# VectorE takes the residual additions of a step between the products and the scans of the next unit

## Chip, cores and metric

The kernel runs on one core of a Trainium2 chip. The metric is the device time of one execution in microseconds (us); lower is better. Before the change the median of three runs is 1209.81 us (1209.77 to 1210.84).

## What is computed

A decoder layer on x of shape (4, 512, 512): a selective state-space block (Mamba), a cross-attention to a context, and an int8-quantized linear layer, each added to x and followed by a layer norm.

```python
proj = einsum('blh,he->bel', x, W_in); hidden, gate = split(proj)
hidden = silu(causal_conv(hidden) + conv_bias)
dt, Bm, Cm = split(hidden.T @ W_x)
dts = softplus(dt @ W_dt + b_dt)
dA  = exp(dts[..., None] * A);  dBu = dts[..., None] * Bm[:, :, None, :] * hidden[..., None]
state = dA[t] * state + dBu[t];  y[t] = einsum('ben,bn->be', state, C[t])      # 512 steps t
x = layernorm(x + ((y + hidden * D) * silu(gate)) @ W_out)
q, k = ctx @ Wq.T + bq, ctx @ Wk.T + bk
x = layernorm(x + x @ softmax(q @ k.T).T)
x = layernorm(x + dequantized(int8(x) @ int8(weight).T) + bias)
```

## The kernel before

**Units and steps.** A batch has E = 1024 channels with N = 16 states each. One unit is 32 channels with all their states: 128 partitions by NJ = 4 rows of T = 512. A batch has 32 units, so there are 128 in all. The program is a table of steps (b, g) with b from -1 to 4 and g from 0 to 31, and every engine walks the same table. In step (b, g) VectorE works on unit u = 32b + g + 1 of the scan; I call it the unit of step g of batch b.

**Five engines on a unit.** SyncE copies the step sizes and inputs of the unit to all partitions (`rep`, L358). ScalarE computes dA = exp (four instructions at L598, for the unit after the present one) and copies the inputs to PSUM (`du_rep`, L606), once VectorE has done the products of the unit before. VectorE multiplies `du_rep` by B into `dBu` (two instructions, L811, "the products") and scans (two instructions, L817). GpSimd multiplies the states by C (two instructions, L466). TensorE sums the states of four units into one product per 128 channels, the key `y` (L945 and L951, function `state_sum`, at g a multiple of 4). VectorE's `finish` (L795, at g = 1, 5, 9, ...) gates that sum.

**The ring.** The states lie in `st`, a ring of RING = 6 units. From the seventh unit on, VectorE's products of unit u wait until TensorE has summed the unit that lay there. For the unit of step g = 4m + 1 that is the sum `y` of step 4m, the step before.

**The dense work beside the scan.** Each step also has items, listed by `items(b, g)` from the tables REST, REST_BESIDE and REST_AFTER: products of TensorE that ScalarE, VectorE or both read. They belong to the batch before (output projection `wo`, scores `en`, attention `at` and `av`, int8 product `ff`), to the gate of the present batch (`g`), or to the batch after (`h`, `c`, `z`, `dt`, `bc`). The four residual kinds are `wo` (g = 2, 5, 6, 7), `av` (15, 17, 19, 21), `ff` (19, 21, 23, 25) and, in the last batch, the early part of its own output projection, `wp` (27 to 30). VectorE adds each of these products to a row block of x: one SCALAR_TENSOR_TENSOR with a row sum (L776, function `add_rows`), or TENSOR_TENSOR (L892) for `wp`; `ff` is scaled first (L903). After it, ScalarE takes the moments in the next step, GpSimd the rstd, and ScalarE normalizes. The numeral behind a kind is the row block: `wo3` is the fourth.

**Three banks.** All dense products share BANKS = 3 PSUM banks in strict turn, in the order of the items. TensorE starts product n only when product n - 3 has been read:

```python
def bank_of(key):
    slot, n = turn[key]
    if n:
        pe.wait_ge(s_free[slot], n)
    return bank(key), s_full[slot]
```

For a residual it is VectorE that gives the bank back, by `dve.sem_inc(free, 1)` behind the addition (L895 and L906). TensorE takes its items in order, so a product that waits for its bank holds up all behind it. For the residual `wo3` the product three places on is the state sum `y` of step 8. For the last batch's loop (b = 3, the dense work is batch 2's) the products three places behind `av0`, the first `ff` and the third `ff` are the state sums of steps 16 and 20 and the gate of step 23; in the loops b = 1 and 2 they are the state sums of steps 16, 20 and 24.

**VectorE's order in a step**, before: products and scans of the unit (`unit(u)`), `finish`, the norms' small parts, and then the items of the step in their order, residuals among them.

Of the kernel before, what the change touches and what calls it, by code (L numbers as in the profile page):

```python
# [5 lines left out]
ALU = mybir.AluOpType  # L6
# [6 lines left out]
NB = 4  # L13
# [13 lines left out]
UNITS = NE * NQ  # L27
TT = T // P
# [91 lines left out]
def decoder_layer(nc, x, xT, ctxT, w_in, w_conv, conv_k, conv_b, w_x, w_dt, b_dt, w_out, a_log, d_skip,  # L120
# [10 lines left out]
    with ExitStack() as ctx:  # L131
# [25 lines left out]
        ws_bc = sb("ws_bc", [P, H])  # L157
# [32 lines left out]
        rows_of = [x1[:]] * LAST + [hs_spare[:, KH:2 * KH, :]]  # L190
# [101 lines left out]
        def product_read(eng, key):  # L292
            slot, n = turn[key]
            eng.wait_ge(s_free[slot], n + 1)
# [458 lines left out]
        def _(dve):  # L753
            V = nc.vector
            chain = [0]

            def link(ins):

                chain[0] += 1
                ins.then_inc(s_chain, 1)  # L760
                dve.wait_ge(s_chain, chain[0])

            def full(key):
                product_done(dve, key)
                return bank(key), s_free[turn[key][0]]
# [5 lines left out]
            def add_rows(key, x_i, ps):  # L771

                n = norm[key]
                if n >= 4:
                    normalized(dve, norm_keys[n - 4])
                V.scalar_tensor_tensor(x_i, ps, 1.0, x_i, ALU.mult, ALU.add,  # L776
                                       accum_out=rowsum[:, n % 4:n % 4 + 1]).then_inc(s_sum, 1)
                dve.wait_ge(s_sum, n + 1)
# [18 lines left out]
                dve.wait_ge(s_y, NE * b + e + 1)  # L797
                dve.sem_inc(free, 1)  # L798

            def unit(u):  # L800
                dve.wait_ge(s_duf, u + 1)
                B = spread_at(dve, u, s_bb, 0, Bb)
                if u >= RING:

                    n = (u - RING) // NQ
                    product_done(dve, ("y", n // NE, n % NE))
                for h in range(NH):
                    j = slice(JH * h, JH * h + JH)
                    if u:
                        dve.wait_ge(s_scan, NH * (u - 1) + h + 1)  # L810
                    V.tensor_tensor(dBu[:, j, :], du_rep[:].unsqueeze(1).to_broadcast([P, JH, T]), B[:, j, :],  # L811
                                    ALU.mult).then_inc(s_mul, 1)
                for h in range(NH):
                    j = slice(JH * h, JH * h + JH)
                    dve.wait_ge(s_mul, NH * u + h + 1)
                    dve.wait_ge(s_dA, NJ * u + JH * (h + 1))
                    V.tensor_tensor_scan(st[:, u % RING, j, :].rearrange("p j t -> p (j t)"),  # L817
                                         dA[:, u % 2, j, :].rearrange("p j t -> p (j t)"),
                                         dBu[:, j, :].rearrange("p j t -> p (j t)"), 0.0,
                                         ALU.mult, ALU.add).then_inc(s_scan, 1)  # L820

            def quantize_weight():

# [24 lines left out]
            V.tensor_scalar(Aneg[:], Aneg[:], -1.0, None, ALU.mult).then_inc(s_prep, 1)  # L848

            norms = {}  # L850
            for s, (b, g) in enumerate(STEPS):
                if 0 <= UNITS * b + g + 1 < NB * UNITS:
                    unit(UNITS * b + g + 1)
                if b == -1 and g == 28:
                    quantize_weight()
                n = NE * b + g // 4 - 1
# [18 lines left out]
                        V.reciprocal(xinv[:, i:i + 1], sc).then_inc(s_xi, 1)  # L875
                for kind, kb, i in items(b, g):
                    key = (kind, kb, i)
                    x_i = rows_of[kb][:, i, :] if kind in ("wp", "wo", "av", "ff") else None
                    if kind == "h" and kb == 0:
                        hid_front(kb, i)  # L880
                    elif kind == "en":
                        ps, _ = full(key)
                        if i >= 2:
                            dve.wait_ge(s_ex, TT * kb + i - 1)
                        V.tensor_reduce(nmax[:, i % 2:i % 2 + 1], ps, AX_X, ALU.max, negate=True).then_inc(s_mx, 1)
                        norms.setdefault(s + 1, []).append(key)
                    elif kind in ("wp", "wo", "av"):
                        if kind in ("wp", "wo") and i == 0:
                            dve.wait_ge(s_xr, 16 * (kb + 1))
                        ps, free = full(key)  # L890
                        if kind == "wp":
                            link(V.tensor_tensor(x_i, ps, x_i, ALU.add))  # L892
                        else:
                            add_rows(key, x_i, ps)
                        dve.sem_inc(free, 1)  # L895
                        if kind == "av":
                            norms.setdefault(s + QUANT_LAG, []).append(key)
                    elif kind == "ff":
                        ps, free = full(key)
                        if kb == 0 and i == 0:  # L900
                            product_read(dve, ("ws", 0, 0))

                        link(V.scalar_tensor_tensor(ps, ps, xsc[:, i:i + 1], ws_bc[:], ALU.mult, ALU.mult))  # L903
                        dve.wait_ge(s_xb, TT * kb + i + 1)
                        add_rows(key, x_i, ps)
                        dve.sem_inc(free, 1)  # L906

        @block.tensor
        def _(pe):
# [187 lines left out]
```

## Time and profile before

| | |
|---|---|
| median of 3 runs | 1209.81 us |
| the profiled execution | 1212.85 us; span 1211.1 us |
| VectorE busy | 974.8 us, 80% |
| TensorE busy | 866.9 us, 72% |
| ScalarE busy | 855.8 us, 71% |
| GpSimd busy | 814.6 us, 67% |
| granted TensorE clock, mean | 0.856 of 2.4 GHz |

The span runs from the first to the last instruction, and the profiled execution's own time is 1.7 us above it. The scans of the 128 units lie between about 75 and 1155 us; before that come the first batch's projections, and behind it the last batch's dense work. In the rows, DVE is VectorE, ACT ScalarE, POOL GpSimd, PE TensorE, and a trailing q is an engine's instruction queue (its waits and semaphore updates).

### The profile page before, as it was taken

The page shows a single profiled execution, that of the slowest core. Times are in us where ns is not written, and L with a number is a line of the kernel's source. Part 1 is how long each engine was busy: PE and PEld are TensorE (multiplying, and loading weights), DVE is VectorE, ACT ScalarE, POOL GpSimd, SP SyncE. Part 2 cuts the span into 40 slices and gives each one's busy share as a digit, 9 for nine tenths or more (in the row PEclk, how much of TensorE's full clock was granted, in tenths as well). Part 3 has the DMA queues.
Part 4 walks back from the last instruction along what each step waited for, and adds up shares of the span by engine and source line. Part 5 has one row for each costly group of instructions (what it writes and reads, how often), then busy time and mean ns, then how long its engine had stood idle before and what let it go on. Part 6 is the DMA issues. An engine that isn't in the chain of part 4 may idle for free.

```text
span 1211.1 us, 10560 instructions
## 1 busy us (share of the span) xinstructions
PE 866.9 (72%) x2718; PEld 339.3 (28%) x2718; DVE 974.8 (80%) x783; ACT 855.8 (71%) x1458; POOL 814.6 (67%) x515
## 2 busy tenths in 40 slices
PE   7933488878368789877549788896727946675995
PEld 2221133322023233332114233332202312222331
DVE  2459999987789987778888977887788999999733
ACT  2386777766557887786666886878756788787546
POOL 2238888876667776686767766868766777777533
PEclk9966699988679889988869899998977978778996
DMA  5184444442973334242793332443395353225100
GB/s 172 35 183 113 97 113 113 126 112 55 244 196 74 87 97 112 70 122 74 186 271 91 85 97 73 103 117 92 89 249 165 72 140 87 59 70 156 27 0 35
DMA packets 66684, 135.03 MB, mean 111 GB/s; under 512 B 13120, under 2 KB 19392, under 8 KB 66624
## 3 DMA queue, kind: packets, MB, share of 16 engines
q1 hardware_dynamic: 65904, 134.28, 43.5%
q8 instruction: 22, 0.36, 0.1%
q14 instruction: 38, 0.31, 0.1%
q10 hardware_dynamic: 720, 0.08, 0.0%
HBM read 62.75 MB, written 4.46 MB: 55 GB/s over the span
## 4 chain that ended last, share of the span: by engine, by line
PE 27%; issue 24%; ACT 18%; DVE 18%; DMA 5%; POOL 4%; SPq 2%; DVEq 0%; ACTq 0%; POOLq 0%
PE dense L919 18%; DVE st L817 12%; PE dense L974 6%; ACT dA L598 5%; POOL st L466 3%; DMA rep<-steps 2%; DVE dBu L811 2%; PE dense L951 2%; DMA wide<-w_out 1%; ACT squares L629 1%; DVE hs L795 1%; SPq L358 1%; ACT du_rep L606 1%; ACT tb L588 1%; PE dBu L929 1%
## 5 line engine op out<-in xcount | busy, mean ns | idle before, releaser
L466 POOL TENSOR_TENSOR st<-st,Cb 128x1024 f32<-128x1024 f32 x250 | 584.4, 2359 | 180.9 <-DVE st L817 153.5
L817 DVE TENSOR_TENSOR_SCAN st<-dA,dBu 128x1024 f32<-128x1024 f32 x256 | 570.2, 2269 | 0.3 <-ACT dA L598 0.3
L598 ACT ACTIVATE dA<-rep,Aneg 128x511 f32<-128x511 f32 x512 | 327.7, 710 | 82.0 <-DMA rep<-steps 51.6
L811 DVE TENSOR_TENSOR dBu<-du_rep,Bb 128x1024 f32<-128x1024 f32 x250 | 294.6, 1224 | 91.8 <-ACT du_rep L606 60.6
L919 PE MATMUL dense<-xTs,Win 128*128 128x512 f32 x512 | 242.2, 618 | 16.6 <-DMA xTs<-xT 7.7
L919 PE MATMUL dense<-wide,hs 128*128 128x512 f32 x256 | 122.2, 634 | 57.9 <-DVE hs L795 34.3
L919 PEld LDWEIGHTS dense<-xTs,Win 128*128 128x128 f32 x512 | 99.1, 198 | 154.2 <-issue 153.5
L974 PE MATMUL dense<-pj,Win 128*128 128x512 f32 (+1 forms) x192 | 106.1, 704 | 47.0 <-DVEq L798 21.2
L951 PE MATMUL dense<-st,sel 128*32 128x512 f32 x1024 | 124.3, 629 | 2.9 <-POOL st L466 2.9
L606 ACT COPY du_rep<-rep 128x512 f32<-128x512 f32 x128 | 74.4, 581 | 41.2 <-DVE dBu L811 39.4
L945 PE MATMUL dense<-hs,Ddiag 128*128 128x512 f32 x64 | 41.2, 731 | 81.9 <-ACT Ddiag L676 72.2
L511 POOL TENSOR_TENSOR ta<-ta,tb 128x512 f32<-128x512 f32 x32 | 41.1, 1284 | 73.5 <-ACT tb L714 71.3
L919 PEld LDWEIGHTS dense<-wide,hs 128*128 128x128 f32 x256 | 51.2, 204 | 127.3 <-issue 65.0
L497 POOL TENSOR_TENSOR steps<-tb,ta 128x512 f32<-128x512 f32 x32 | 40.6, 1270 | 54.4 <-ACT tb L588 54.4
L974 PEld LDWEIGHTS dense<-pj,Win 128*128 128x128 f32 x192 | 42.6, 231 | 108.3 <-issue 108.3
L480 POOL TENSOR_TENSOR hs<-tb,ta 128x512 f32<-128x512 f32 x32 | 40.7, 1272 | 39.6 <-ACT tb L558 39.6
L937 PE MATMUL dense<-ident,small 128*128 128x128 f32 x128 | 25.2, 333 | 46.7 <-ACT small L647 26.7
L951 PEld LDWEIGHTS dense<-st,sel 128*32 128x32 f32 x1024 | 31.1, 116 | 97.5 <-issue 84.8
L711 ACT ACTIVATE tb<-dense 128x512 f32<-128x512 f32 x32 | 18.9, 592 | 55.1 <-PE dense L919 54.7
L776 DVE SCALAR_TENSOR_TENSOR x<-dense,x 128x512 f32<-128x512 f32 x36 | 24.7, 687 | 36.1 <-PE dense L919 29.0
L919 PE MATMUL dense<-hs,wide 128*128 128x512 f32 x80 | 43.6, 702 | 10.3 <-issue 9.6
L472 POOL TENSOR_TENSOR rstd<-var,neghalf 128x1 f32<-128x1 f32 x48 | 26.5, 551 | 36.0 <-ACT var L632 36.0
(117 smaller groups left out, 998.4 us busy)
## 6 DMA issues: line engine op xcount, KB each, us to landing
rep<-steps SPq DMA_DIRECT2D x512, 128.0 KB, 2.7
Win<-w_in SPq DMA_DIRECT2D x64, 256.0 KB, 2.7
wide<-w_out SPq DMA_DIRECT2D x4, 2048.0 KB, 14.0
Win<-w_conv SPq DMA_DIRECT2D x24, 256.0 KB, 2.7
wide<-bc_rows SPq DMA_DIRECT2D x24, 256.0 KB, 6.5
xTs<-xT SPq DMA_DIRECT2D x4, 1024.0 KB, 10.9
Bb<-bc_rows SPq DMA_DIRECT2D x16, 256.0 KB, 10.8
Cb<-bc_rows SPq DMA_DIRECT2D x16, 256.0 KB, 11.8
```

Source lines behind the costliest of these rows:

```text
L466: nc.gpsimd.tensor_tensor(s, s, C[:, j, :], ALU.mult).then_inc(s_p, 1)
L480: nc.gpsimd.tensor_tensor(hs[:, kb % 2, i, :], tb[:, m, :], ta[:, m, :], ALU.mult).then_inc(s_hs, 1)
L497: nc.gpsimd.tensor_tensor(steps[:, n % 3, 0, :], t, a, ALU.add).then_inc(s_dt, 1)
L511: nc.gpsimd.tensor_tensor(a, a, t, ALU.mult).then_inc(s_gate, 1)
L598: nc.scalar.activation(dA[:, u % 2, j, 1:T], rep[:, u % REPS, 0, 1:T], ACT.Exp, scale=Aneg[:, u % UNITS, j:j + 1]).then_inc(s_dA, 1)
L606: nc.scalar.copy(du_rep[:], rep[:, u % REPS, 1, :]).then_inc(s_duf, 1)
L811: V.tensor_tensor(dBu[:, j, :], du_rep[:].unsqueeze(1).to_broadcast([P, JH, T]), B[:, j, :], ALU.mult).then_inc(s_mul, 1)
L817: V.tensor_tensor_scan(st[:, u % RING, j, :].rearrange("p j t -> p (j t)"), dA[:, u % 2, j, :].rearrange("p j t -> p (j t)"), dBu[:, j, :] ...
L919: mm = nc.tensor.matmul(ps[0:rows, :], lhsT, rhs, start=n == 0, stop=n == len(pairs) - 1)
L945: nc.tensor.matmul(ps, Ddiag[:], hs[:, b % 2, e, :], start=True, stop=False)
L951: mm = nc.tensor.matmul(ps[32 * q:32 * q + 32, :], sel[:, 0:32], st[:, (4 * n + q) % RING, j, :], start=False, stop=j == NJ - 1)
L974: mm = nc.tensor.matmul(ps[:, k:T], Win[:, n % 3, k, :], pj[:, 0:T - k], start=k == 0, stop=k == KC - 1)
```

## The change

`unit` is split into `products` and `scans`. An item of a residual kind is no longer done in its place: its key goes into the list `late`, and the next step does it between the products and the scans of its unit. Steps without a unit (the tail behind the last scan) do it at their start. The other engines' programs are the same, instruction by instruction.

```diff
-            def unit(u):
+            def products(u):
                 dve.wait_ge(s_duf, u + 1)
                 B = spread_at(dve, u, s_bb, 0, Bb)
                 if u >= RING:
...
+
+            def scans(u):
+
                 for h in range(NH):
...
+            def residual(key):
+
+                kind, b, i = key
+                x_i = rows_of[b][:, i, :]
+                if kind in ("wp", "wo") and i == 0:
+                    dve.wait_ge(s_xr, 16 * (b + 1))
+                ps, free = full(key)
+                if kind == "wp":
+                    link(V.tensor_tensor(x_i, ps, x_i, ALU.add))
+                elif kind == "ff":
...
+                    link(V.scalar_tensor_tensor(ps, ps, xsc[:, i:i + 1], ws_bc[:], ALU.mult, ALU.mult))
+                    dve.wait_ge(s_xb, TT * b + i + 1)
+                    add_rows(key, x_i, ps)
+                else:
+                    add_rows(key, x_i, ps)
+                dve.sem_inc(free, 1)
...
+            late = []
             for s, (b, g) in enumerate(STEPS):
                 if 0 <= UNITS * b + g + 1 < NB * UNITS:
-                    unit(UNITS * b + g + 1)
+                    products(UNITS * b + g + 1)
+                for key in late:
+                    residual(key)
+                late = []
+                if 0 <= UNITS * b + g + 1 < NB * UNITS:
+                    scans(UNITS * b + g + 1)
...
-                    elif kind in ("wp", "wo", "av"):
...
+                    elif kind in ("wp", "wo", "av", "ff"):
+                        late.append(key)
                         if kind == "av":
                             norms.setdefault(s + QUANT_LAG, []).append(key)
-                    elif kind == "ff":
...
```

VectorE's order before, from step 6 to step 9 of the loop b = 1: L811 are the products, L817 the scans, L776 the residuals `wo2` (bank dense1) and `wo3` (bank dense0), L885 the score maximum of `en0`.

```order
L811 TENSOR_TENSOR dBu<-du_rep,Bb 128x1024 x2
L817 SCALAR_TENSOR_TENSOR st<-dA,dBu 128x1024 x2
L776 SCALAR_TENSOR_TENSOR x1,rowsum<-dense1,x1 128x512
L811 TENSOR_TENSOR dBu<-du_rep,Bb 128x1024 x2
L817 SCALAR_TENSOR_TENSOR st<-dA,dBu 128x1024 x2
L776 SCALAR_TENSOR_TENSOR x1,rowsum<-dense0,x1 128x512
L811 TENSOR_TENSOR dBu<-du_rep,Bb 128x1024 x2
L817 SCALAR_TENSOR_TENSOR st<-dA,dBu 128x1024 x2
L885 TENSOR_REDUCE nmax<-dense2 128x1
```

And in the changed kernel, over the same steps (the scans now have line L820, the score maximum L913):

```order
L811 TENSOR_TENSOR dBu<-du_rep,Bb 128x1024 x2
L776 SCALAR_TENSOR_TENSOR x1,rowsum<-dense1,x1 128x512
L820 SCALAR_TENSOR_TENSOR st<-dA,dBu 128x1024 x2
L811 TENSOR_TENSOR dBu<-du_rep,Bb 128x1024 x2
L776 SCALAR_TENSOR_TENSOR x1,rowsum<-dense0,x1 128x512
L820 SCALAR_TENSOR_TENSOR st<-dA,dBu 128x1024 x2
L913 TENSOR_REDUCE nmax<-dense2 128x1
L811 TENSOR_TENSOR dBu<-du_rep,Bb 128x1024 x2
L820 SCALAR_TENSOR_TENSOR st<-dA,dBu 128x1024 x2
```

Each residual has moved past the two products of the next unit, and so has the return of its bank.

The second place is the turn from step 23 to step 24 of the loop b = 3. Before, VectorE scales and adds the third `ff` (bank dense2), takes two score maxima, and then does the products:

```order
L903 SCALAR_TENSOR_TENSOR dense2<-dense2,xsc,ws_bc 128x512
L776 SCALAR_TENSOR_TENSOR x1,rowsum<-dense2,x1 128x512
L885 TENSOR_REDUCE nmax<-dense0 128x1
L885 TENSOR_REDUCE nmax<-dense1 128x1
L811 TENSOR_TENSOR dBu<-du_rep,Bb 128x1024 x2
L817 SCALAR_TENSOR_TENSOR st<-dA,dBu 128x1024 x2
```

In the changed kernel (L838 is the scaling):

```order
L913 TENSOR_REDUCE nmax<-dense0 128x1
L913 TENSOR_REDUCE nmax<-dense1 128x1
L811 TENSOR_TENSOR dBu<-du_rep,Bb 128x1024 x2
L838 SCALAR_TENSOR_TENSOR dense2<-dense2,xsc,ws_bc 128x512
L776 SCALAR_TENSOR_TENSOR x1,rowsum<-dense2,x1 128x512
L820 SCALAR_TENSOR_TENSOR st<-dA,dBu 128x1024 x2
```

The third `ff` now stands behind the maxima and behind the products of step 24.

## Rows read from the trace of the kernel before

**Rows 1.** The page, part 4: the chain that ended last, shares by engine.
```profile
PE 27%; issue 24%; ACT 18%; DVE 18%; DMA 5%; POOL 4%; SPq 2%; DVEq 0%; ACTq 0%; POOLq 0%
```

**Rows 2.** Waits of VectorE: who waited for whom: us in total, times, longest.
```profile
DVE x L776 <- PE dense L919: 29.0, 5, 7.2
DVE dense L903 <- PE dense L919: 14.7, 6, 4.8
```

**Rows 3.** Timeline of VectorE, b = 1, steps 2 to 17: start, us, instruction, [idle before].
```profile
352.72 0.69 DVE L776 SCALAR_TENSOR_TENSOR x<-dense,x 128x512 f32<-128x512 f32 x1 [2.86 <-PE dense L919]
...
353.67 2.37 DVE L811 TENSOR_TENSOR dBu<-du_rep,Bb 128x1024 f32<-128x1024 f32 x2 [0.24 <-PE dense L919]
355.94 4.45 DVE L817 TENSOR_TENSOR_SCAN st<-dA,dBu 128x1024 f32<-128x1024 f32 x2
361.71 2.36 DVE L811 TENSOR_TENSOR dBu<-du_rep,Bb 128x1024 f32<-128x1024 f32 x2 [1.31 <-ACT du_rep L606]
...
473.03 2.36 DVE L811 TENSOR_TENSOR dBu<-du_rep,Bb 128x1024 f32<-128x1024 f32 x2 [0.72 <-PE dense L951]
```

**Rows 4.** Timeline of VectorE, b = 1, steps 7 to 9.
```profile
391.89 0.67 DVE L776 SCALAR_TENSOR_TENSOR x<-dense,x 128x512 f32<-128x512 f32 x1
...
393.01 2.36 DVE L811 TENSOR_TENSOR dBu<-du_rep,Bb 128x1024 f32<-128x1024 f32 x2 [0.44 <-ACT du_rep L606]
...
400.23 2.35 DVE L811 TENSOR_TENSOR dBu<-du_rep,Bb 128x1024 f32<-128x1024 f32 x2
```

**Rows 5.** Timeline of TensorE, b = 1, the state sum of step 8.
```profile
392.68 2.07 PE L945 MATMUL dense<-hs,Ddiag 128*128 128x512 f32 x2 [2.94 <-DVEq L895]
394.68 4.11 PE L951 MATMUL dense<-st,sel 128*32 128x512 f32 x32
```

**Rows 6.** Chain in order of time, b = 2, steps 7 to 9.
```profile
679.75 2.07 PE dense L945 x2
681.82 5.56 PE dense L951 x32
...
687.51 0.10 DVE dBu L811
```

**Rows 7.** Timeline of ScalarE: its copies to du_rep behind residuals, b = 1 and 3.
```profile
526.39 0.59 ACT L606 COPY du_rep<-rep 128x512 f32<-128x512 f32 x1 [1.18 <-DVE dBu L811]
...
1079.62 0.59 ACT L606 COPY du_rep<-rep 128x512 f32<-128x512 f32 x1 [1.67 <-DVE dBu L811]
```

**Rows 8.** Timeline of TensorE, b = 3: state sums of steps 16 and 20, gate of step 23.
```profile
1027.61 3.64 PE L951 MATMUL dense<-st,sel 128*32 128x512 f32 x32
...
1060.72 3.64 PE L951 MATMUL dense<-st,sel 128*32 128x512 f32 x32
...
1093.07 3.67 PE L919 MATMUL dense<-xTs,Win 128*128 128x512 f32 x8 [2.08 <-DVEq L906]
```

**Rows 9.** Timeline of VectorE, b = 3, steps 15 to 29.
```profile
1026.69 2.36 DVE L811 TENSOR_TENSOR dBu<-du_rep,Bb 128x1024 f32<-128x1024 f32 x2 [0.24 <-ACT du_rep L606]
...
1033.33 2.34 DVE L811 TENSOR_TENSOR dBu<-du_rep,Bb 128x1024 f32<-128x1024 f32 x2
...
1056.92 0.69 DVE L776 SCALAR_TENSOR_TENSOR x<-dense,x 128x512 f32<-128x512 f32 x1
...
1066.16 2.34 DVE L811 TENSOR_TENSOR dBu<-du_rep,Bb 128x1024 f32<-128x1024 f32 x2
...
1091.39 0.74 DVE L903 SCALAR_TENSOR_TENSOR dense<-dense,xsc,ws_bc 128x512 f32<-128x512 f32 x1
...
1094.64 2.36 DVE L811 TENSOR_TENSOR dBu<-du_rep,Bb 128x1024 f32<-128x1024 f32 x2 [0.34 <-ACT du_rep L606]
...
1140.33 2.36 DVE L811 TENSOR_TENSOR dBu<-du_rep,Bb 128x1024 f32<-128x1024 f32 x2 [3.83 <-PE dense L951]
```

**Rows 10.** Timeline of ScalarE, b = 3: du_rep of step 19, gate of step 23.
```profile
1057.39 0.58 ACT L606 COPY du_rep<-rep 128x512 f32<-128x512 f32 x1
...
1097.14 0.60 ACT L711 ACTIVATE tb<-dense 128x512 f32<-128x512 f32 x1 [0.17 <-ACT xTs L739]
```

More of the change, by code:

```diff
@@ L820, in unit @@
                                          ALU.mult, ALU.add).then_inc(s_scan, 1)
+            def residual(key):
[7 more added lines that the diff above has]
+                elif kind == "ff":
+                    if b == 0 and i == 0:
+                        product_read(dve, ("ws", 0, 0))
+                    link(V.scalar_tensor_tensor(ps, ps, xsc[:, i:i + 1], ws_bc[:], ALU.mult, ALU.mult))
[4 more added lines that the diff above has]
+                dve.sem_inc(free, 1)
             def quantize_weight():
@@ L877, in _ @@
                     key = (kind, kb, i)
-                    x_i = rows_of[kb][:, i, :] if kind in ("wp", "wo", "av", "ff") else None
                     if kind == "h" and kb == 0:
@@ L886, in _ @@
                         norms.setdefault(s + 1, []).append(key)
-                    elif kind in ("wp", "wo", "av"):
[L888 to L895, printed above, removed]
+                    elif kind in ("wp", "wo", "av", "ff"):
+                        late.append(key)
                         if kind == "av":
                             norms.setdefault(s + QUANT_LAG, []).append(key)
-                    elif kind == "ff":
[L899 to L906, printed above, removed]
         @block.tensor
```

## Prediction

> **What bounds the kernel now.** I read the views in this order: the chain that ended last, VectorE's waits, then the timelines of VectorE, TensorE and ScalarE at every residual. No engine bounds the span alone: the chain is shared by TensorE, ScalarE and VectorE, with "issue" for the rest [rows 1]. VectorE's waits for the product that a residual adds come to 29.0 + 14.7 us [rows 2]. So each step ends on whichever wait is last there, and the change has to be priced place by place. There are 52 residuals; 12 lie in the tail, where no unit is left and VectorE's order stays the same, and one more (the last `wp`) is followed by a step without a unit. The other 39 stand at 33 turns of a step.
>
> **What the change moves.** No instruction is added. A residual that started right behind the scans now starts 2.27 us after the next products start, since 355.94 - 353.67 is what the products hold VectorE [rows 3]. A plain residual takes 0.95 us of VectorE (353.67 - 352.72) [rows 3]. The products are issued earlier, the residual later, the scans as before if both were ready. Nothing is moved past SyncE's or GpSimd's queue. Three things can then happen.
>
> **1. A wait for TensorE is covered.** `wo0` in three loops, `av0` twice, `av2`/`ff0` twice and the third `ff` twice wait for their product longer than the products take: 2.86 us in the row shown, up to 7.2 [rows 2, 3]. There the scans start about 2.3 us earlier, nine times. But what the next step waits for is not VectorE's. Behind `wo0` the next products already wait 1.31 us for `du_rep` [rows 3], which ScalarE copies only after it has read TensorE's later products; behind `av0` they wait 0.72 us for the state sum [rows 3], and I take the two `ff` places to be alike. I cost this gain at nothing; what covers it is TensorE's own run of products, and if that were faster the whole 2.3 us would count.
>
> **2. ScalarE gets its copy earlier.** Where ScalarE was waiting for VectorE's products, the products now come before the residual. Behind `av3`/`ff1` the copy waited 1.18 us in the loops b = 1 and 2 and 1.67 us in b = 3 [rows 7], and there the chain runs through ScalarE. Gain 2 x 1.18 = **2.4 us** in the first two; the third is used in item 3. The bounds are 0 and 2.4: nothing else of size waits there.
>
> **3. The bank comes back later, and TensorE waits.** This is the term that decides. The release goes from the end of the residual before the products to 2.27 us and one residual after their start. Where `n + 3` starts later than that anyway it costs nothing: `wo0`, `av1`, `av3`, `ff1`, all of `av0`, `ff0`, `ff2` in the first two loops, and `wo1`/`wo2`, whose delay only moves products that ScalarE or VectorE come to later still. It costs at these places:
>
> State sum of step 8, three loops. TensorE already stood idle 2.94 us for the bank of `wo3` and began 0.79 us after the residual did (392.68 - 391.89) [rows 4, 5]. Now the products start when `du_rep` is there, 393.01; the residual at 395.28; the sum at 396.07, 3.39 us later. It ended at 394.68 + 4.11 = 398.79 and will at 402.2. By the ring the products of step 9 need it: 402.3 instead of 400.23, +2.1 us. In b = 2 the sum was already what those products waited for (679.75 to 687.38, then 687.51) [rows 6], so all 3.4 us count. The same sum took 6.1 us in one loop and 7.6 in the other [rows 5, 6], so lengths are unsure: if each takes 7.6, it is 3.6 + 3.4 + 3.6 = 10.6; if each takes 6.1, it is 2.1 + 1.9 + 2.1 = 6.1. The loop b = 3 has rows as b = 1. I take **8.2**, near the middle, since I have one row of each length.
>
> State sum of step 16, b = 3. The release lay just before the products at 1026.69 [rows 9] and goes 3.0 us back. The sum ended at 1031.25 [rows 8] and will at 1034.3; the next products started at 1033.33 [rows 9] and will at 1034.4: +1.0. If the sum takes 7.6 us as in rows 6 instead of its 4.7 here, +3.9. I take **1.9**.
>
> State sum of step 20, b = 3. The pair began at 1056.92 [rows 9]. Now the products begin with `du_rep`, copied by 1057.97 [rows 10], and the pair at 1060.24, 3.3 us later. The sum ended at 1064.36 [rows 8], will at 1067.7, and the next products come at 1067.7 instead of 1066.16 [rows 9]: I take **1.4**, bounds 1.0 and 4.0 by the same slower sum.
>
> Gate of step 23, b = 3. TensorE waited 2.08 us for the bank of the third `ff` and started at 1093.07 [rows 8]; ScalarE read the gate at 1097.14, just as it was full [rows 10]. Now the products wait for `du_rep` until 1094.64, and the `ff` starts at 1096.91 instead of 1091.39 [rows 9]: 5.5 us later, and the gate is in front of ScalarE's next exps and copy. The 1.67 us of item 2 bring `du_rep` forward, of which I keep 1.1, because the norm there also waits for GpSimd. Net 4.4. Bounds: 3.5, if the whole head start counts and a little slack is left, and 7.6, if the gate's 3.67 us double at half clock. I take **4.5**.
>
> `wp1`, b = 3. It was done in a 3.83 us wait for the state sum [rows 9]; behind the products it delays the scans by its whole **0.95 us**, bounds 0.9 and 2.6 (its bank). Small ones at the third loop's `ff3`: 0.3.
>
> Sum: 8.2 + 1.9 + 1.4 + 4.5 + 0.95 + 0.3 - 2.4 = **+14.9 us**. With all lower ends (6.1 + 1.0 + 1.0 + 3.5 + 0.9 - 2.4) it is +10.1, with all upper ends and no gain (10.6 + 3.9 + 4.0 + 7.6 + 2.6 + 0.3) +29.0.
>
> **The clock.** The state sum at 392.68 came after 2.94 us of TensorE standing idle and took 6.1 us, the one at 679.75 took 7.6 [rows 5, 6]; the one at 1060.72 ran at 3.64 us for its L951 part, against 5.56 [rows 6, 8]. The change makes the idle stretches longer, hence the slower ends above. The Trainium skill ("TensorE: Matmul & The Clock Gate", section "What's actually happening") says that the throttled clock is the default and that activity releases it. By that rule every delayed product would run at the lower clock, and the sum would be near the +29 of the upper ends; the row of 6.1 us agrees only in part.
>
> **Rivals.**
> *A, the queue is cleared (faster).* VectorE's queue is in order, so a residual whose product is late holds products that are ready. If ScalarE's copy follows VectorE's products closely after `wo0`, `av0`, `ff0` and `ff2`, each of the nine places gives 2.3 us and the gains of item 2 are kept: -20.7 - 2.4 = -23, or 1186.8 us. It decides as soon as `du_rep` of the next unit comes over 2.3 us earlier than now. For it: 43.7 us of such waits [rows 2]. Against: `du_rep` is the later one behind `wo0` [rows 3]. The Trainium skill states the same order ("TensorE: Matmul & The Clock Gate", "Architectural detail: the array is 16× 32×32, not 1× 128×128"): VectorE's queue is strictly first in, first out. By that rule alone the change wins.
> *B, the banks are not felt (no change).* TensorE's delay is absorbed by slack that the chain does not show. Then only VectorE's own shifts remain: three times 0.9 us behind `wo3` (the residual no longer fills the 0.44 us wait and what lay before it), 0.8 and 1.1 at steps 15 and 19, 0.95 at `wp1`, minus 2.4 and the rest of item 2: +1.5, or 1211.3 us. For it: step 9 had 1.4 us of slack in b = 1. Against: the chain of b = 2 goes through that very sum [rows 6], and TensorE was waiting for the release [rows 5].
> *C, everything slower.* The low clock holds after each new gap: +25 to +29, about 1237. The Trainium skill ("Perfetto Trace Analysis", section "Matmuls") wants products to rotate through banks so that reading one overlaps the next; here the reading is put off with only three banks. It speaks for my sign, not for a size.
> That the change does nothing is ruled out: the order of 39 residuals is different.
>
> **How the numbers follow.** The forecast has 0.72, A 0.07, B 0.13, C 0.08. The profiled execution took 1212.85 us, 3.0 above the median; its sum gives 1227.8, and against the median of 1209.81 us it is 1224.7 us. About 0.2% (2.4 us) is what the measurement can tell from no change. The range must leave out at most 2 in 10: it drops A and most of B at the low end and most of C at the top, 1212 to 1232. Faster: A and a sliver of B, 0.08. Same: most of B, 0.11. Slower: 0.81.
>
> **What would show it.** Right: TensorE's idle time before L945 behind VectorE's release grows; the products of step 9 wait for L951 in all three loops; the state sum of step 8 starts over 3 us later relative to the end of the scans of step 7; VectorE's waits for L919 at the residuals shrink by up to 20 us while its waits for `du_rep` or L951 grow by more; between steps 22 and 25 of b = 3 the changed kernel loses 4 us or more; the tail behind 1166 us is as long as before. Wrong: if TensorE's waits for VectorE's release don't grow, or if steps 7 to 10 take as long as before, item 3 fails.

## The result, and the profile after

The changed kernel took 1228.28 us (median of 4 runs, 1224.77 to 1229.41), the kernel before beside it 1210.32 us (4 runs, 1209.77 to 1211.04): ratio 1.0143, 95% interval 1.0121 to 1.0165, so **slower by 18.0 us**. The forecast was 1224.7 us, with a range of 1212 to 1232.

The two profiled executions lie closer together, 1224.77 against 1212.85 us: that of the changed kernel is its fastest run, and that of the kernel before is longer than all its others here. They already differ by 3.8 us at the first products of b = 1, where both programs are still the same. Counted from there the change costs 15.7 us in the traces.

The chain that ended last, of the changed kernel (the page, part 4), against [rows 1]:

```profile
PE 29%; issue 22%; ACT 19%; DVE 15%; POOL 6%; DMA 6%; SPq 2%; DVEq 0%; ACTq 0%; POOLq 0%
```

VectorE went down by three points and TensorE up by two. VectorE's waits (us in total, times, longest):

```profile
DVE dBu L811 <- ACT du_rep L606: 93.8, 44, 8.8
...
DVE dBu L811 <- issue: 14.3, 4, 8.0
DVE dBu L811 <- PE dense L963: 13.4, 8, 3.0
...
DVE x L776 <- PE dense L931: 6.0, 5, 1.5
DVE dense L838 <- PE dense L931: 5.6, 5, 3.3
```

The last two answer to [rows 2]: VectorE now waits 11.6 us for late products and not 43.7. The change does what it says. But it waits elsewhere: 93.8 us for ScalarE's copy (63.8 before) and 13.4 us for the state sum, L963 (5.3 before). The reason is on TensorE. Its waits for VectorE's signal that a bank is free (L843 is the residual's `sem_inc`):

```profile
PE dense L931 <- DVEq L843: 17.7, 9, 8.4
PE dense L957 <- DVEq L843: 15.8, 6, 4.1
```

Before, the state sum waited 9.7 us for such signals. The state sums of step 8, in the order of the loops (TensorE's timeline: start, us, instruction, [idle before]):

```profile
391.95 2.08 PE L957 MATMUL dense<-hs,Ddiag 128*128 128x512 f32 x2 [4.07 <-DVEq L843]
393.95 5.69 PE L963 MATMUL dense<-st,sel 128*32 128x512 f32 x32
...
682.54 2.07 PE L957 MATMUL dense<-hs,Ddiag 128*128 128x512 f32 x2 [4.07 <-DVEq L843]
684.54 5.46 PE L963 MATMUL dense<-st,sel 128*32 128x512 f32 x32
...
968.57 2.07 PE L957 MATMUL dense<-hs,Ddiag 128*128 128x512 f32 x2 [4.08 <-DVEq L843]
970.57 4.11 PE L963 MATMUL dense<-st,sel 128*32 128x512 f32 x32
```

TensorE stands idle 4.1 us in front of each, 2.94 us before in b = 1 [rows 5]. VectorE around the first of them:

```profile
388.87 2.36 DVE L811 TENSOR_TENSOR dBu<-du_rep,Bb 128x1024 f32<-128x1024 f32 x2 [1.05 <-ACT du_rep L606]
391.15 0.68 DVE L776 SCALAR_TENSOR_TENSOR x<-dense,x 128x512 f32<-128x512 f32 x1
...
392.05 4.46 DVE L820 TENSOR_TENSOR_SCAN st<-dA,dBu 128x1024 f32<-128x1024 f32 x2 [0.21 <-DVE x L776]
...
399.78 2.36 DVE L811 TENSOR_TENSOR dBu<-du_rep,Bb 128x1024 f32<-128x1024 f32 x2 [2.68 <-issue]
```

The residual starts 2.28 us after the products and the sum 0.80 us after the residual, as the working had it. The sum ends at 399.64, and the next products at 399.78 stood 2.68 us idle for it. In [rows 4] they had nothing to wait for.

The gate of step 23 in b = 3, on TensorE's timeline:

```profile
1101.22 5.39 PE L931 MATMUL dense<-xTs,Win 128*128 128x512 f32 x8 [8.41 <-DVEq L843]
```

VectorE around it:

```profile
1097.26 2.37 DVE L811 TENSOR_TENSOR dBu<-du_rep,Bb 128x1024 f32<-128x1024 f32 x2 [0.60 <-ACT du_rep L606]
1099.53 0.75 DVE L838 SCALAR_TENSOR_TENSOR dense<-dense,xsc,ws_bc 128x512 f32<-128x512 f32 x1
...
1111.60 2.36 DVE L811 TENSOR_TENSOR dBu<-du_rep,Bb 128x1024 f32<-128x1024 f32 x2 [5.80 <-ACT du_rep L606]
```

ScalarE, where it reads the gate:

```profile
1106.65 0.60 ACT L711 ACTIVATE tb<-dense 128x512 f32<-128x512 f32 x1 [7.06 <-PE dense L931]
```

These answer to the last rows of [rows 8, 9, 10]: idle time of 2.08 us became 8.41, and the gate took 5.39 us, not 3.67, at a granted clock of 0.67, where it had been 1.00. ScalarE, which read it without waiting for TensorE, now waits 7.06 us, and behind it VectorE waits 5.80.

`wp1` and `wp2`, near the end of b = 3: TensorE now waits 2.60 us for the bank that `wp2` takes, where before it went on at once (24 matmuls here are `wp2` and `wp3` together):

```profile
1154.32 10.68 PE L931 MATMUL dense<-wide,hs 128*128 128x512 f32 x24 [2.60 <-DVEq L843]
```

Where the time went, in us, by the difference (after minus before) of the moment at which a unit's first product ended. "Lost" is the change of that difference over the stretch:

| stretch | difference | lost | forecast |
|---|---|---|---|
| first products of b = 1 | -3.8 | | |
| step 8 to 9, b = 1 | -4.1 to -0.4 | 3.7 | 2.1 to 3.6 |
| rest of b = 1 | -0.4 to -0.4 | 0 | -1.2 |
| step 8 to 9, b = 2 | -0.6 to 2.6 | 3.2 | 1.9 to 3.4 |
| rest of b = 2 | 2.6 to -0.4 | -3.0 | -1.2 |
| step 8 to 9, b = 3 | -0.6 to 1.5 | 2.1 | 2.1 to 3.6 |
| to step 17, b = 3 | 1.5 to 2.6 | 1.1 | 1.9 |
| to step 21, b = 3 | 2.6 to 4.0 | 1.4 | 1.4 |
| step 23 to 25, b = 3 | 4.0 to 9.7 | 5.7 | 4.5 |
| from there to the tail | 9.7 to 11.8 | 2.2 | 1.25 |

### The profile page after: what moved, and what is told of

Same layout as the page of the kernel before. It is cut to its first block, busy times and chain, and to the rows that moved or that the text cites. A ratio compares the mean times of both kernels' runs of the same rounds, so it can differ in the third digit from the quotient of the medians.

```text
span 1222.9 us, 10550 instructions
## 1 busy us (share of the span) xinstructions
PE 864.8 (71%) x2708; PEld 338.0 (28%) x2718; DVE 976.5 (80%) x783; ACT 855.8 (70%) x1458; POOL 814.6 (67%) x515
## 3 DMA queue, kind: packets, MB, share of 16 engines
HBM read 62.75 MB, written 4.46 MB: 55 GB/s over the span
## 4 chain that ended last, share of the span: by engine, by line
PE 29%; issue 22%; ACT 19%; DVE 15%; POOL 6%; DMA 6%; SPq 2%; DVEq 0%; ACTq 0%; POOLq 0%
PE dense L931 18%; DVE st L820 9%; ACT dA L598 6%; PE dense L986 6%; POOL st L466 4%; PE dense L963 3%; DVE dBu L811 3%; DMA wide<-w_out 2%; ACT du_rep L606 1%; DMA rep<-steps 1%; ACT squares L629 1%; ACT tb L588 1%; DMA Bb<-bc_rows 1%; DVE hs L795 1%; PE dense L957 1%
## 5 line engine op out<-in xcount | busy, mean ns | idle before, releaser
L820 DVE TENSOR_TENSOR_SCAN st<-dA,dBu 128x1024 f32<-128x1024 f32 x256 | 570.4, 2269 | 7.4 <-DVE x L776 6.4
L811 DVE TENSOR_TENSOR dBu<-du_rep,Bb 128x1024 f32<-128x1024 f32 x250 | 294.5, 1224 | 139.8 <-ACT du_rep L606 90.4
L963 PE MATMUL dense<-st,sel 128*32 128x512 f32 x1024 | 126.0, 636 | 2.9 <-POOL st L466 2.9
L963 PEld LDWEIGHTS dense<-st,sel 128*32 128x32 f32 x1024 | 31.3, 116 | 98.9 <-issue 85.5
L639 ACT ACTIVATE x<-x,nmean,rstd 128x512 f32<-128x512 f32 x36 | 28.9, 814 | 37.3 <-POOL nmean L474 37.3
L931 PE MATMUL dense<-wide 128*128 128x512 f32 x96 | 48.0, 646 | 3.6 <-ACT ta L584 2.5
## 6 DMA issues: line engine op xcount, KB each, us to landing
wide<-w_out SPq DMA_DIRECT2D x4, 2048.0 KB, 14.9
Cb<-bc_rows SPq DMA_DIRECT2D x16, 256.0 KB, 11.8
```

The lines of the kernel that those rows point to most:

```text
L931: mm = nc.tensor.matmul(ps[0:rows, :], lhsT, rhs, start=n == 0, stop=n == len(pairs) - 1)
L963: mm = nc.tensor.matmul(ps[32 * q:32 * q + 32, :], sel[:, 0:32], st[:, (4 * n + q) % RING, j, :], start=False, stop=j == NJ - 1)
```

## The experiments

All versions ran in three jobs, each beside the kernel before: its medians there were 1210.22 us (13 runs), 1211.08 us (19 runs) and 1211.81 us (27 runs), with single runs from 1206.51 to 1217.22. The versions that move some residuals only are the changed kernel with a condition in its last loop:

```diff
-                        late.append(key)
+                        if b < NB and (CONDITION):
+                            late.append(key)
+                        else:
+                            residual(key)
```

where `kb` is the batch of the residual, one less than the loop: `kb < LAST - 1` means the loops b = 1 and 2.

### Only the release is late

The kernel before, with this in place of `dve.sem_inc(free, 1)` behind a residual:

```diff
-                        dve.sem_inc(free, 1)
+                        late.append(free)
...
             def unit(u):
...
+                if late:
+                    dve.wait_ge(s_mul, NH * (u + 1))
+                    returned(late)
                 for h in range(NH):
```

> Every residual stays in its old place behind the scans; only the signal that gives its bank back is sent behind the next unit's products. Theory (the late bank is what costs): the state sum of step 8 and the gate of step 23 in b = 3 start late as in the changed kernel, less the 0.95 us of the residual itself: about 6.5 us for the three state sums, 4.6 us for the gate, 1 to 2 us for the rest, together +12 us against the kernel before (+8 to +18), near 1222 us. Rival (what costs is that VectorE does the residual between products and scans, so that the scans start later): the order on VectorE is the old one, so within 2 us of the kernel before, 1210 us.

Measured: 1225.48 us (4 runs, one of them 1236.2, which widens the interval), ratio 1.0164 (1.0113 to 1.0216). The scans kept their place behind the products, and the time was lost all the same. The edit does one thing more than delay the signal: VectorE waits for the signal of its own products, and so the scans start 2.57 us after the products start, not 2.27:

```profile
375.94 2.36 DVE L816 TENSOR_TENSOR dBu<-du_rep,Bb 128x1024 f32<-128x1024 f32 x2
378.51 4.47 DVE L825 TENSOR_TENSOR_SCAN st<-dA,dBu 128x1024 f32<-128x1024 f32 x2 [0.21 <-DVE dBu L816]
```

From these products to the next ones it took 7.66 us, and 7.56 before. At 33 turns that is 3.3 us at the most, too little for the 15.3. TensorE's waits in this version (L802 is the release, L956 the state sum's first products, L930 among others the gate, L948 products that transpose a block):

```profile
PE dense L930 <- DVEq L802: 16.3, 11, 6.5
PE dense L948 <- DVEq L802: 15.8, 7, 3.8
PE dense L956 <- DVEq L802: 12.3, 6, 3.4
```

The time between the medians is 15.3 us, for the change's 18.0. In the traces it is lost in the same places: 1.7, 1.5 and 1.7 us from step 8 to 9 of the three loops and 5.1 from step 23 to 25 of b = 3. So the rival, that the order of the work on VectorE alone costs the time, falls. It is not shown that the late signal is the whole of the change's loss: the three sums lose 4.9 us here and 9.0 there, where the residual stands in front of the signal as well (the sum starts 3.4 us later behind the scans of step 7, and 2.7 us here) and two of the sums also took longer.

### The release later still

```diff
-                if late:
-                    dve.wait_ge(s_mul, NH * (u + 1))
-                    returned(late)
...
+                    if h == 0 and late:
+                        dve.wait_ge(s_scan, NH * u + 1)
+                        returned(late)
```

> As the version in which only the signal that gives the bank back is late, but the signal now goes out behind the first of the next unit's two scans, 2.2 us later still; the residuals and everything else on VectorE in the old order. Theory: the three state sums, the gate of step 23 and the state sums of steps 16 and 20 of b = 3 start 2.2 us later once more, so 4 x 2.2 = 9 to 6 x 2.2 = 13 us above the first version, near 1236 us, more where slack in the loops b = 1 and 2 is used up. Rival (the cost is one lost turn, not a time that grows with the delay): as the first version, 1225 us.

Measured: 1253.36 us (4 runs), ratio 1.0336 (1.0307 to 1.0364), 41.5 us above the kernel before where 26 were expected. TensorE's waits for the same release:

```profile
PE dense L948 <- DVEq L802: 28.8, 7, 6.3
...
PE dense L930 <- DVEq L802: 24.5, 11, 8.5
PE dense L956 <- DVEq L802: 21.6, 8, 4.0
```

The cost grows with the delay, and faster than in proportion: 2.2 us more at each release turned 15.3 us into 41.5, each against the kernel before of its own job. The size was missed. From step 19 to 25 of b = 1 and b = 2 this version loses 6.4 and 8.8 us, where the first loses nothing; some of it comes back behind step 25. From step 9 to the next loop's first products it loses 4.1 and 5.7 us, where the first gains 1.9 and 0.4. So the clause "more where slack is used up", which had no number, carried 12 of the 28 us between the two traces; the other 16 are more than the 13 expected, too. How much of it is the lower clock (0.843 on the mean, 0.854 in the first version) stays open.

### Only wo

CONDITION `kind == "wo"`.

> Only the wo residuals go behind the next products; av, ff and wp stay in place. Theory: wo3 of three loops is in it and carries 8.7 us, wo0 to wo2 carry nothing; +8.7 us against the kernel before (+6 to +11), near 1219 us, and TensorE's idle time before the gate of step 23 in b = 3 is as before. Rival (each residual carries a like share, for instance through longer waits for du_rep): 11 of the 39 moved residuals, so 11/39 of the 18 us measured, +5 us or less.

Measured: 1219.30 us (4 runs), ratio 1.0085 (1.0062 to 1.0108): +9.1 us for an expected 8.7. Half of the loss comes from 12 of 39 residuals (the expectation counts 11, but there are four in each of three loops; the rival's +5 us would be 5.5). By the trace most of it comes from three of them: +2.2, +3.4 and +2.3 us from step 8 to 9 of the three loops, 7.9 together. From step 21 to 27 of b = 3, with the gate in it, the difference to the kernel before stays within 0.3 us.

### The third ff of b = 3 in its old place

CONDITION `key != ("ff", LAST - 1, 2)`.

> The changed kernel, but the third ff of the loop b = 3 stays behind the scans. Theory (its late bank holds up the gate of step 23): TensorE's idle time before that gate falls from 8.4 us to 2 to 4 us. If the gate then takes 3.67 us the whole 5.5 us come back, near 1223 us; if it takes 6.5 us, as it did with the chosen residuals alone behind 4.29 us of idle time, about 2.5 us come back, near 1226 us. Rival (the late av3/ff1 two steps before is what costs): no change, 1228 us.

Measured: 1226.78 us (4 runs, 1222.61 to 1231.93), ratio 1.0128 (1.0084 to 1.0172), 1.5 us below the changed kernel's 1228.28, which the scatter of the runs doesn't tell from nothing. In the trace the stretch from step 23 to 25 costs 3.1 us less, by the second branch of the expectation:

```profile
1062.84 2.08 PE L960 MATMUL dense<-hs,Ddiag 128*128 128x512 f32 x2 [0.93 <-DVEq L843]
1064.85 5.76 PE L966 MATMUL dense<-st,sel 128*32 128x512 f32 x32
...
1097.68 6.46 PE L934 MATMUL dense<-xTs,Win 128*128 128x512 f32 x8 [4.28 <-DVEq L843]
```

TensorE's idle time halved to 4.28 us, but the gate took 6.46 us. And the state sum of step 20, on which nothing was changed, took 7.8 us and not 4.7, which cost 3.1 us in this execution. So the gate's part is seen in the trace, and the medians neither show nor refute it.

### Chosen residuals

CONDITION `(kind, i) in (("wo", 0), ("av", 3), ("ff", 1)) or kb < LAST - 1 and (kind, i) in (("av", 0), ("av", 2), ("ff", 0), ("ff", 2))`, and in the second version all seven only with `kb < LAST - 1`.

> Moved are only the residuals whose product VectorE waits for longest and those behind which ScalarE waits for its copy, and none whose bank TensorE needs at once: wo0, av3 and ff1 in three loops, av0, av2, ff0 and ff2 in the loops b = 1 and 2 (wo0, av0, av2/ff0 and ff2 have late products). Theory (covered waits give nothing, the copy behind av3/ff1 gives 1.2 us a loop or somewhat more): -2 to -5 us against the kernel before, near 1206.5 us. Rival A of the prediction (VectorE's queue cleared at nine places gives 2.3 us each): of these, eight or nine places are in it, -15 us or more. Rival (these moves only lose): 0 or above.

> Moved are wo0, av0, av2, ff0, av3, ff1 and ff2 in the loops b = 1 and 2 only, nothing in b = 3. Theory: the gain of about 2.2 us a loop behind av3/ff1 stays and the 3.1 us that the earlier copy cost in b = 3 by a slow gate product are not there: -4 to -6 us against the kernel before, near 1205 us. Rival (the gains are the scatter of TensorE's clock): within 2 us of the kernel before.

Measured: the first 1208.24 us (10 runs), ratio 0.9983 (0.9962 to 1.0003), an interval that takes in no change; the second 1206.77 us (10 runs), ratio 0.9960 (0.9934 to 0.9987). The two intervals overlap, so that it is better to leave out b = 3 isn't shown by the medians. What speaks for it is the gate of b = 3, here in the first version:

```profile
1085.42 6.52 PE L934 MATMUL dense<-xTs,Win 128*128 128x512 f32 x8 [4.29 <-DVEq L843]
```

and the granted clock in the gate's stretch. The kernel before (window, its us, TensorE busy, PEclk, DMA share, GB/s):

```profile
1093.10:1096.60 3.50, 3.50 (x9) 1.00 1.01 344
```

The first version, in the same view:

```profile
1085.50:1091.80 6.30, 6.30 (x9) 0.55 1.06 336
```

The same eight matmuls at the same load of the DMA engines took 3.67 us at a granted clock of 1.00, which is 2.4 GHz, and 6.52 us at 0.55, mostly at 1.2 GHz. The earlier copy of ScalarE let TensorE run ahead into a wait of 4.29 us, not 2.08; the stretch from step 23 to 25 then lost 2.7 us in the trace. But in the second version, where nothing is moved in b = 3, the gate was slow too, at a granted clock of 0.67:

```profile
1084.73 5.37 PE L934 MATMUL dense<-xTs,Win 128*128 128x512 f32 x8 [2.51 <-DVEq L843]
```

It lost 1.4 us there. So a part of what the first version lost at its gate may be this scatter.

### Which of the chosen ones gain

Only av3 and ff1: CONDITION `kb < LAST - 1 and (kind, i) in (("av", 3), ("ff", 1))`. Only late products: the same with `wo0`, `av0`, `av2`, `ff0`, `ff2`.

> Only av3 and ff1 of step 21 go behind the next products, in the loops b = 1 and 2: four residuals. Theory (the gain of the chosen version is ScalarE's earlier copy, and the residuals with a late product give nothing): the same as that version, -3 to -5 us against the kernel before, near 1206.5 us. Rival A of the prediction (VectorE's queue, held by late products, is what is cleared): under half of it, 0 to -2 us.

> Only the residuals whose product VectorE waits for go behind the next products, in the loops b = 1 and 2: wo0, av0, av2, ff0 and ff2, at eight places of a step. Theory: what the next step waits for is not VectorE's, so each earlier scan is given back in the following step: 0, within 1.5 us of the kernel before. Rival A of the prediction: 2.3 us at each of the eight, up to -18 us; any part of it above 2 us speaks for it.

Measured: av3 and ff1 1208.13 us (11 runs), ratio 0.9974 (0.9951 to 0.9997), 3.7 us below the kernel before's 1211.81; the late products 1212.71 us (11 runs), ratio 0.9996 (0.9975 to 1.0016). The two intervals overlap a little, and the traces tell the two apart: from step 21 to 25 of b = 1 and b = 2, behind av3 and ff1, the first gains 2.3 and 2.0 us and the second nothing within 0.1, and over all that follows the first products of b = 1 the second gains 0.7 us. So four residuals bring the gain, and the ten others next to nothing. In the trace of the second, VectorE behind `wo0`:

```profile
345.74 2.34 DVE L811 TENSOR_TENSOR dBu<-du_rep,Bb 128x1024 f32<-128x1024 f32 x2
348.32 0.69 DVE L776 SCALAR_TENSOR_TENSOR x<-dense,x 128x512 f32<-128x512 f32 x1 [0.24 <-PE dense L934]
...
349.23 4.47 DVE L820 TENSOR_TENSOR_SCAN st<-dA,dBu 128x1024 f32<-128x1024 f32 x2 [0.21 <-DVE x L776]
357.30 1.23 DVE L811 TENSOR_TENSOR dBu<-du_rep,Bb 128x1024 f32<-128x1024 f32 x1 [3.61 <-ACT du_rep L606]
```

The 2.86 us of [rows 3] are down to 0.24, the scan starts earlier, and the next wait for `du_rep` is 3.61 us, not 1.31. From scan to next products it now takes 8.1 us, not 5.8: the gain is given back. What `du_rep` waits for is on ScalarE:

```profile
349.10 0.69 ACT L583 ACTIVATE tb<-dense,bdt 128x512 f32<-128x512 f32 x1 [4.74 <-PE dense L934]
...
356.70 0.57 ACT L606 COPY du_rep<-rep 128x512 f32<-128x512 f32 x1
```

ScalarE stands 4.74 us for TensorE's product (4.92 before) and then works without a pause up to the copy. The gain of av3 and ff1 is seen, in the trace of the version with these alone, on ScalarE:

```profile
521.29 0.58 ACT L606 COPY du_rep<-rep 128x512 f32<-128x512 f32 x1
...
525.75 0.58 ACT L606 COPY du_rep<-rep 128x512 f32<-128x512 f32 x1
```

and on TensorE, at the last convolution product of step 23:

```profile
536.67 5.17 PE L989 MATMUL dense<-pj,Win 128*128 128x512 f32 x8 [3.96 <-ACT pj L566]
```

Two copies follow each other after 4.46 us, not after 5.74 (520.65 to 526.39 before): 1.28 us, near the 1.18 of [rows 7]. The other 1.0 us of this loop's 2.3 is TensorE's: in the kernel before the same product took 6.21 us behind 5.54 of idle time. That part is less sure, as the changed kernel shows in the same place:

```profile
535.29 6.74 PE L986 MATMUL dense<-pj,Win 128*128 128x512 f32 x8 [3.95 <-ACT pj L566]
```

Nine of the kept traces have av3 and ff1 moved in both loops. From step 21 to 25, 15 of these 18 loops gain 2.0 to 2.5 us; the others are the changed kernel's with 0.8 and 3.1 and the second chosen version's first with 3.3.

### All but wo3, in two loops

CONDITION `kb < LAST - 1 and (kind, i) != ("wo", 3)`.

> In the loops b = 1 and 2 all residuals but wo3 go behind the next products, in b = 3 none; against the chosen version wo1, wo2, av1 and ff3 are moved as well, which the prediction costed at nothing but for 0.3 us in b = 3. Theory: as the chosen version, within 1.5 us, near 1207 us. Rival (these residuals also hold a bank that TensorE needs): 1 us or more for each of the eight, 1214 us or above.

Measured: 1205.10 us (10 runs, 1200.32 to 1212.27), ratio **0.9944 (0.9921 to 0.9967)**. This is the fastest version: faster than both kernels, 6.7 us below the kernel before. That it beats the chosen ones isn't shown, since the intervals overlap and its profiled execution (span 1205.9 us against 1204.2 for the second of them) doesn't say so. `wo1`, `wo2`, `av1` and `ff3` cost nothing that shows, as forecast.

### The state sum on another bank

Three versions change the order in which TensorE does its products, and so who gets which bank: the state sum ahead of `en0` in step 8 (on the changed kernel), also `h0` ahead of `en1` in step 9, and both with the chosen residuals of two loops.

```diff
+    if 1 <= b < NB and g == 8:
+        keys.insert(0, keys.pop())
+    if 1 <= b < LAST and g == 9:
+        keys.append(keys.pop(0))
     return keys
```

> The changed kernel, but in step 8 of the loops b = 1 to 3 TensorE does the state sum ahead of the score product en0, so that the sum takes the bank of z, long free, and en0 the bank of wo3. Theory: the 8.7 us of the three state sums go, and what the kernel before lost there by its 2.9 us of TensorE's idle time may go too: 8 to 12 us less than the changed kernel, near 1218.5 us, while the gate of step 23 in b = 3 is as late as before. Rival (the sum is late for another reason, VectorE's or GpSimd's results): no more than 2 us less than the changed kernel, 1226 to 1229 us.

> The version with the state sum first, and in step 9 of the loops b = 1 and 2 also h0 ahead of the score product en1, so that h0 takes the gate's bank and no longer that of the state sum, for which TensorE stood idle 10.52 us and ran h0 in 5.58 us instead of 3.60. Theory (the bank wait had moved from the sum to h0 and gave the gain back): 3 to 5 us less than the version with the sum first, about 1219 us, 8 to 10 us less than the changed kernel; VectorE then waits about 1.2 us for en1 twice. Rival (the gain was lost elsewhere, by a slower TensorE clock in steps 11 to 13): no difference to the version with the sum first, 1223 us.

> The same chosen residuals of the loops b = 1 and 2, with the state sum first in step 8 of three loops and h0 ahead of en1 in step 9 of two. Theory: in the kernel before TensorE stood idle 2.94 us for the bank of wo3 in front of a sum of 6.2 to 7.6 us, and the products of step 9 waited for it in b = 2; 1 to 2 us a loop go, so that it stands 6 to 10 us below the kernel before, near 1202 us. Rival (in the kernel before the sum is late for nothing that matters): as the version without the new order of products, near 1205 us.

Measured: 1222.93 us (4 runs; 1.0114, 1.0092 to 1.0136), 1228.07 us (4 runs; 1.0141, 1.0102 to 1.0180) and 1211.09 us (10 runs; 1.0009, 0.9988 to 1.0029). All three missed: 5.4 us below the changed kernel and not 8 to 12, none and not 8 to 10, none below the kernel before and not 6 to 10. The first, on TensorE:

```profile
386.81 1.02 PE L959 MATMUL dense<-hs,Ddiag 128*128 128x512 f32 x2
387.77 3.64 PE L965 MATMUL dense<-st,sel 128*32 128x512 f32 x32
...
404.47 5.58 PE L933 MATMUL dense<-xTs,Win 128*128 128x512 f32 x8 [10.52 <-DVEq L800]
```

The sum does start 5 us earlier and takes 4.6 us, not 7.7, and the products of step 9 gain 2.8, 2.5 and 1.2 us. But `h0` now follows the sum on its bank and waits 10.52 us for `finish` (L800); ScalarE stands 4.1 us for it, and 3.3 us go back in steps 10 to 13 of b = 1 and of b = 2. In the second version it is `en1` that follows, on TensorE:

```profile
408.88 2.08 PE L935 MATMUL dense<-small 128*128 128x512 f32 x2 [7.86 <-DVEq L802]
```

and on VectorE:

```profile
411.00 0.69 DVE L917 TENSOR_REDUCE nmax<-dense 128x1 f32<-128x512 f32 x1 [1.92 <-PE dense L935]
```

VectorE needs `en1` in the same step and waits 1.92 us for it. That is +2.0 us at step 10 in both loops against the first version, and 3.3 us come back, as reckoned; over these steps the trace is 1.3 us a loop better. That the whole is 5 us worse between the medians (4.3 against the kernels before of their jobs, and 11 between the traces) comes from elsewhere: 3.8 us up to the first unit's products, and pieces of 1.6 to 1.7 us at single later steps. What of this is the version's doing stays open. With three banks a late one could be handed on, but not got rid of.

## Why the prediction was right

**The sign and the mechanism.** Item 3, "the bank comes back later, and TensorE waits", was the term that decides, and the late release alone brings 15.3 us. The residual's start behind the products (2.28 us for a forecast 2.27) and the sum's behind the residual (0.80 for 0.79) were as in the working; the sum of step 8 starts 3.42 us later behind the scans of step 7, for a forecast 3.39, and the tail is as long as before. VectorE's waits for late products shrank by 32.1 us, though, more than the "up to 20" of the forecast's signs, and its waits for `du_rep` and the state sum grew by 38.1.

**State sum of step 8.** Forecast 8.2, in the traces 9.0, with `wo` alone 7.9 in its trace and 9.1 us in the medians. The choice to take one row of each length was near: the three sums took 7.7, 7.5 and 6.1 us.

**Steps 16 and 20 of b = 3.** 1.9 and 1.4 forecast, 1.1 and 1.4 found: both sums ran at full clock, the lower end of the first.

**The gate of step 23.** 4.5 forecast, 5.7 found. The step that was short is the gate's own time: I kept 3.67 us and put the slower gate only into the bound (which is too low by its own terms: 4.4 and 3.67 more are 8.1, not 7.6). It took 5.39 us behind 8.41 us of idle time. To undo it gave back 3.1 us in the trace, since the gate was slow there behind half of that idle time, too.

**wp1 and ff3.** 1.25 forecast, 2.2 found: 1.3 us by the first products of the last unit, and 0.9 us on the way into the tail. The bank, which I had in the bound only, was late too.

**Item 1, costed at nothing.** Shown for the loops b = 1 and 2: with the late products alone the time is 0.9996 of the kernel before (0.9975 to 1.0016). Rival A (1186.8 us) falls. Its condition, `du_rep` over 2.3 us earlier, isn't met: in that trace the products of the next unit come at most 0.4 us earlier. Behind `wo0` ScalarE's copy waits for TensorE's products and not for VectorE, and behind the first `av0` it is the state sum that the products wait for, 3.01 us. The rule of the Trainium skill that VectorE's queue is first in, first out ("TensorE: Matmul & The Clock Gate", section "Architectural detail: the array is 16× 32×32, not 1× 128×128") agrees with the rows, where products moved ahead of a late residual do start earlier; it says nothing on whether anybody waits for them.

**Item 2, 2.4 us.** 3.0 us over the rest of the two loops in the change's traces, 3.7 us alone in the medians. It was under-sized, 1.2 us a loop for the 2.0 to 2.5 that most traces show: TensorE's shorter idle time and, mostly, its faster product come on top of the 1.28 us. That the change's own traces come near the forecast is partly luck, since b = 1 gave nothing on balance (0.8 us from step 21 to 25) and b = 2 all of the 3.0.

**Rival B** (1211.3 us) falls by the waits for L843. **Rival C**, the low clock everywhere (about 1237), holds in part: of the five delayed sums three ran slowly and two at full clock, and the gate was slow. The three slow ones are those of step 8, which had run slowly before, too (6.1, 7.6 and 6.3 us). The Trainium skill describes a clock that goes up and down when TensorE idles between groups of products that cycle through banks, and the loss of throughput with it ("TensorE: Matmul & The Clock Gate", section "A second HAM failure mode: psum-queue depth-cycling"). The rows agree in kind: granted 0.55 behind 4.29 us of idle time, 1.00 behind 2.08. But it took 0.67 behind 2.51 us in one version and 0.67 behind 8.41 in the changed kernel, so the idle time in front doesn't settle it by itself.

**The sum** was 14.9 us for 15.7 in the traces and 18.0 between the medians. It is that near because the misses partly cancel: +1.2 us at the gate, +0.9 at `wp1`, +0.8 at step 8 and -0.8 at step 16, 0.6 more of gain from item 2, and 0.7 that came back between the stretches of the table. What makes up the last 2.3 us isn't settled: it is less than single executions of one version differ by.

## What to carry to other kernels

When a reader is moved behind other work, its release moves too: list who gets each released buffer next, and when. With a short rotation that price is paid on the other engine, and here it grew faster than the delay: 2.2 us more turned 15.3 into 41.5. A wait that disappears brings time only where the next wait is for the same engine; here 4 of 14 moved residuals carried nearly the whole gain, and leaving out those whose bank is wanted at once (wo3), with all of b = 3, turned 1.4% slower into 0.6% faster. Moving the late buffer to another user by reordering needs the same list again for that user.

## What the runs showed of the hardware

The same products of TensorE take very different times, and small shifts of the program around them decide it. The gate's eight matmuls, with the same instructions on TensorE before them, took 3.67 us at a granted clock of 1.00 in six traces, each behind 1.1 to 2.1 us of idle time. They took 5.3 to 6.5 us in the eight others, behind 2.5 to 8.5 us, at 0.55 to 0.69. The length doesn't grow with the idle time: 6.52 us came behind 4.29, 5.39 behind 8.41, and 5.37 behind 2.51 in a version that moves nothing in b = 3. So an idle stretch of 2.2 us more could cost these 2.2 us and 2.8 us more of a slower product, and a version that brings TensorE forward by a little can lose by it. The scatter is larger than I had taken it to be: the kernel before ran from 1206.51 to 1217.22 us in the later jobs, and even ten runs a side left intervals of 0.2 to 0.3% to each side, 2.5 to 3 us.
